# A second attention's gathers, its last tiles and its first ones: who issues, who sums, and in what order

## The reference

```python
kv_scores, indices = _pk(x, Wq_pk, pk_keys)      # per token and head: 16 best of 128 x 128 product keys, and their softmax
ind = indices + offsets[None, None, :, None]     # offsets = head * 128 * 128
k = jnp.einsum('bnhk,bnhkd->bnhd', kv_scores, keys_table[ind])
v = jnp.einsum('bnhk,bnhkd->bnhd', kv_scores, values_table[ind])
sim = jnp.einsum('bihd,bjhd->bhij', q, k)        # q is scaled by 128 ** -0.5
sim = jnp.where(causal, sim, neg)
attn = jax.nn.softmax(sim, axis=-1)
out = jnp.einsum('bhij,bjhd->bhid', attn, v)     # then heads side by side, times Wo, added to x
```

## Time and profile before

| | us |
|---|---|
| median of 3 runs | 2843.3 (2838.46, 2843.3, 2846.46) |
| the profiled execution, device time | 2838.24 |
| its span, first to last instruction | 2836.3 |
| mean granted TensorE clock | 0.932 of full speed |

### The profile page before, as it was taken

The page is one execution under the profiler, slowest core; times in us unless marked ns, Lnnn a source line. Parts: engine busy times, 40 slices in busy tenths (PEclk is TensorE's granted clock), DMA queues, the critical chain, the costliest instruction groups (busy, mean ns, idle before and its releaser), DMA issues. The chain is left out here.

```text
span 2836.3 us, 47902 instructions
## 1 busy us (share of the span) xinstructions
PE 2195.5 (77%) x11489; PEld 1773.8 (63%) x11489; DVE 1867.1 (66%) x6336; ACT 783.3 (28%) x2063; POOL 1931.2 (68%) x2033
## 2 busy tenths in 40 slices
PE   6948678887788777886878767877788777877777
PEld 6948556766566556665666655665566655665565
DVE  6689777766666666657566665656666666666541
ACT  5746422221122212221222212221223112221222
POOL 0003767777777777777777777777777777777773
PEclk8969889999999899999899899998999989989999
DMA  4301333333333333333333333333333333333332
GB/s 154 108 1 30 91 95 108 111 108 108 107 111 108 109 108 111 107 108 109 107 110 109 109 107 111 109 110 107 108 110 108 109 108 110 108 109 107 107 108 74
DMA packets 116173, 293.47 MB, mean 103 GB/s; under 512 B 37600, under 2 KB 49248, under 8 KB 113792
## 3 DMA queue, kind: packets, MB, share of 16 engines
q0 software_dynamic: 96816, 264.50, 32.6%
q1 hardware_dynamic: 14880, 23.22, 2.5%
q10 hardware_dynamic: 4144, 2.17, 0.3%
HBM read 288.69 MB, written 1.05 MB: 102 GB/s over the span
## 5 line engine op out<-in xcount | busy, mean ns | idle before, releaser
L321 POOL DMA_INDIRECT ring<-table,rows x2017 | 1923.6, 954 | 707.4 <-issue 578.3
L1565 PE MATMUL ps<-ring,staged 128*128 128x256 f32 x4096 | 995.8, 400 | 191.0 <-DMA ring<-table,rows 169.8
L1565 PEld LDWEIGHTS ps<-ring,staged 128*128 128x128 f32 x4096 | 806.0, 200 | 355.4 <-DMA ring<-table,rows 212.1
L807 DVE RECIPROCAL prec<-psum_row 128x1 f32<-128x1 f32 x128 | 21.0, 164 | 502.1 <-DVEq L806 501.8
L1641 PE MATMUL ps<-s2w,work 128*128 128x128 f32 x2176 | 306.2, 288 | 34.6 <-PEq L1639 33.8
L1177 ACT ACTIVATE work<-ps 128x256 f32<-128x256 f32 x128 | 49.0, 383 | 978.6 <-ACTq L1175 978.6
L1641 PEld LDWEIGHTS ps<-s2w,work 128*128 128x128 f32 x2176 | 274.3, 198 | 64.7 <-issue 61.2
L1610 PE MATMUL ps<-work,qT 128*128 128x512 f32 (+3 forms) x576 | 242.8, 552 | 70.4 <-PEq L1602 67.0
L799 DVE TENSOR_REDUCE nmax<-ps 128x1 f32<-128x128 f32 (+7 forms) x127 | 162.7, 1281 | 204.2 <-DVEq L798 203.5
L792 DVE TENSOR_TENSOR staged<-ps,wgt 128x2048 f32<-128x2048 f32 x128 | 292.0, 2281 | 0.2 <-issue 0.2
L1628 PE MATMUL ps<-ident,work 128*128 128x128 f32 x1088 | 189.8, 298 | 41.9 <-PEq L1551 21.7
(11 more groups left out here) (246 smaller groups left out, 2583.3 us busy)
## 6 DMA issues: line engine op xcount, KB each, us to landing
ring<-table SPq DMA_DIRECT2D x3968, 1.0 KB
ring<-table,rows POOLq DMA_INDIRECT x2017, 2.7
staged<-adj_in SPq DMA_DIRECT2D x16, 1024.0 KB, 4.8
xs<-x_in SPq DMA_DIRECT2D x4, 256.0 KB, 6.6
wpkq<-w_pkq ACTq DMA_DIRECT2D x7, 128.0 KB
out<-xs SPq DMA_DIRECT2D x1, 832.0 KB, 4.8
keyd<-pk_keys ACTq DMA_DIRECT2D x14, 32.0 KB
wo<-w_o ACTq DMA_DIRECT2D x7, 64.0 KB, 2.0
```

The costliest lines, as they stand in the source:

```text
L321: nc.gpsimd.indirect_dma_start(ring[:, t % RING, k, :], None, table_d, bass.IndirectOffsetOnAxis(ap=rows[:, t % ROWS, k:k + 1], axis=0),). ...
L1565: ins = m.matmul(to, diag(t)[:, k, :], ring[:, t % RING, k, :], start=(k == 0), stop=(k == TOPK - 1))
```

## The change

It has five parts.

1. GpSimd issues all 16 gathers of every tile, in one loop over all heads. `fetch_rows`, `turn_offsets`, `offsets_out`, `rowl` and `offs` go. The sixteenth gather of tile 15 counts on a semaphore of its own (`last_in`), so the waits have the same totals in each head.
2. SP issues the weight loads of heads 1 to 7, in place of ScalarE. It waits for `head_used` (ScalarE, in the projection of tile 15) and for `wo_used` (VectorE, as before).
3. At the start ScalarE does `elu_exp(3)` and `exp_best(3)` ahead of `kv_out(0)`, and the projection of tile 5 and the keys of tile 0 ahead of the rest of groups 3 and 4. TensorE does step 0's work right behind the sum of tile 0, then groups 3 and 4. VectorE does `spread(1)` between `elu_in(4)` and `elu_out(4)`.
4. In the last head tiles 14 and 15 are summed by VectorE: for each k one instruction multiplies the gathered rows by the token's weight and adds the sum so far, which stands in PSUM (`weighted`). There is no spread for them.
5. Tile 15's softmax is done in two parts. The past 1920 columns get their own maximum, exponential, turned blocks and product with the output weights; the own 128 columns follow with the maximum of all, and both results are added to the residual with factors that bring them to one scale (`old_scale`, `f_past`, `f_own`). The results leave in three DMAs.

```diff
@@ SP
+            with sp.Fori(1, HEADS) as h:
+                sp.wait_ge(head_used, 1)
+                sp.sem_inc(head_used, -1)
+                load_head(h)
+                sp.wait_ge(wo_used, 1)
+                sp.sem_inc(wo_used, -1)
+                sp.dma_start(wo[:, :], wo_d[h]).then_inc(wo_in, 16)
...
@@ GpSimd
-                for k in range(TOPK - by_rows(t, first)):
+                for k in range(TOPK):
...
@@ VectorE
             elu_in(4)
-            elu_out(4)
-            normal(4)
...
+            spread(1)
+            elu_out(4)
             weigh(AHEAD - 1)
+            normal(4)
             v.drain()
-            for t in range(T):
+            for t in range(1, T):
                 step(t, True, False)
...
+            def weighted(t, q):
+
+                landed(t, q)
+                for k in range(q * QK, (q + 1) * QK):
+                    w, row = wgt[:, t % 4, k:k + 1], ring[:, t % RING, k, :]
+                    if t == T - 1 and k == TOPK - 1:
+                        dve.wait_ge(last_in, 16 * HEADS)
+                    if k == 0:
+                        v.tensor_scalar(end_ps, row, w, None, ALU.mult)
+                    elif k < TOPK - 1:
+                        v.scalar_tensor_tensor(end_ps, row, w, end_ps, ALU.mult, ALU.add)
+                    else:
+                        v.scalar_tensor_tensor(kv[:, t, :], row, w, end_ps, ALU.mult, ALU.add).then_inc(kv_full, 1)
+                    v.drain()
...
+            for t in range(T - 2):
                 step(t, False, True)
+            add_out(T - 4)
+            weighted(T - 2, 0)
+            score_max(T - 3)
+            for q in range(1, QUARTERS):
+                weighted(T - 2, q)
+            score_max(T - 2)
+            add_out(T - 3)
+            dve.sem_inc(out_ready, 1)
+            weighted(T - 1, 0)
             dve.wait_ge(s_full, 1)
             dve.sem_inc(s_full, -1)
+            v.reduce_max(max_past, ps[:, 4:8, :].rearrange("p b n -> p (b n)")[:, 0:(T - 1) * P], X,
+                         negate=True).then_inc(nmax_full, 1)
+            weighted(T - 1, 1)
+            weighted(T - 1, 2)
+            add_out(T - 2)
+            dve.sem_inc(out_ready, 1)
+            weighted(T - 1, 3)
...
@@ ScalarE
+            elu_exp(3)
+            exp_best(AHEAD - 1)
             kv_out(0)
-            for g in (3, 4):
-                elu_exp(g)
-                norm_root(*GROUPS[g])
-                rows_in(g)
-                group_out(g)
...
+                softmax(t - 2)
+                turned_out(t - 2, PARITY[t - 2], t - 1)
+                softmax(t - 1)
+                turned_block(t - 1, PARITY[t - 1], 0)
+                turned_block(t - 1, PARITY[t - 1], 1)
+                act.wait_ge(nmax_full, 1)
+                act.sem_inc(nmax_full, -1)
+                s.activation(row[:, 0:past], scored[:, 0:past], ACT.Exp, bias=max_past, accum_out=sum_past).then_inc(prob_full, 1)
+                turned_block(t - 1, PARITY[t - 1], 2)
+                turned_block(t - 1, PARITY[t - 1], 3)
+                output_turned()
...
+            project_out(AHEAD + 1)
+            key_out(0)
+            norm_root(*GROUPS[3])
+            rows_in(3)
+            elu_exp(4)
+            group_out(3)
+            norm_root(*GROUPS[4])
+            rows_in(4)
+            group_out(4)
...
@@ TensorE
+            def last_steps():
+                t = T - 2
+                exponentials()
+                past_scores(t)
+                values(t - 1, PARITY[t - 1], bank1, key=t)
+
+                t = T - 1
+                exponentials()
+                past_scores(t).then_inc(s_full, 1)
+                values(t - 1, PARITY[t - 1], bank1)
+                exponentials()
+                turn_block(t - 1, PARITY[t], 0, t)
+                bank1()
+                for b in range(3):
+                    turn_block(t - 1, PARITY[t], b + 1, t)
+                    sum_block(t - 1, PARITY[t], b)
+                kv_copied()
+                turn_keys(t, ps[:, 0, 2 * P:3 * P])
+                sum_block(t - 1, PARITY[t], 3).then_inc(ot_full, 1)
+                pe.wait_ge(kt_sb, 1)
+                pe.sem_inc(kt_sb, -1)
+                own_scores(t)
+                output(t)
...
+            project(AHEAD + 1)
+            kv_copied()
+            turn_keys(0)
+            scores(0)
+            group(3)
+            group(4)
```

More of the change, by code:

```diff
@@ L45 @@
 ROWS = 2 * RING
[L46 to L51, removed]
 ROW_SLOTS = (3, 6)
@@ L260, in _ @@
             sp.dma_start(wo[:, :], wo_d[0]).then_inc(wo_in, 16)
[L261 to L273, removed]
-            for t in range(T):
[L276 to L281, removed]
+            with sp.Fori(1, HEADS) as h:
[5 more added lines that the diff above has]
+                sp.dma_start(wo[:, :], wo_d[h]).then_inc(wo_in, 16)
             sp.wait_ge(out_ready, 1)
             o = out_d.rearrange("(t p) d -> p t d", p=P)
-            sp.dma_start(o[:, 0:T - 3, :], xs[:, 0:T - 3, :]).then_inc(out_done, 16)
+            sp.dma_start(o[:, 0:T - 2, :], xs[:, 0:T - 2, :]).then_inc(out_done, 16)
             sp.wait_ge(out_ready, 2)
-            sp.dma_start(o[:, T - 3:T, :], xs[:, T - 3:T, :]).then_inc(out_done, 16)
-            sp.wait_ge(out_done, 32)
+            sp.dma_start(o[:, T - 2, :], xs[:, T - 2, :]).then_inc(out_done, 16)
+            sp.wait_ge(out_ready, 3)
+            sp.dma_start(o[:, T - 1, :], xs[:, T - 1, :]).then_inc(out_done, 16)
+            sp.wait_ge(out_done, 48)
         @block.gpsimd
@@ L323, in gather @@
                         bass.IndirectOffsetOnAxis(ap=rows[:, t % ROWS, k:k + 1], axis=0),
-                    ).then_inc(gathered[t % RING][k // QK], 16)
-            for t in range(T):
-                gather(t, True)
-            with pool.Fori(1, HEADS):
+                    ).then_inc(last_in if t == T - 1 and k == TOPK - 1 else gathered[t % RING][k // QK], 16)
+            with pool.Fori(0, HEADS):
                 for t in range(T):
-                    gather(t, False)
+                    gather(t)
         @block.vector
@@ L938, in _, with landed @@
                     step(t, False, False)
-            for t in range(T):
-                step(t, False, True)
+            def landed(t, q):
+                per = [16 * (QK - (q == QUARTERS - 1 and s == T - 1)) for s in range(t % RING, T, RING)]
+                dve.wait_ge(gathered[t % RING][q], (HEADS - 1) * sum(per) + sum(per[:t // RING + 1]))
+            def weighted(t, q):
[11 more added lines that the diff above has]
+                    v.drain()
@@ L1282, in step @@
+            def step(t, first, last):
                 if not (last and t >= T - AHEAD + 1):
@@ L1692, in step @@
                         bank1()
-                    sums(h, t, range(QUARTERS), first)
+                    sums(h, t)
                     exponentials()
```

309 lines of the change are left out of this document (146 added, 163 removed).

## The result

The changed kernel takes 2861.8 us (median of four runs, 2860.4 to 2862.2), the kernel before in the same measurement 2842.1 us (four runs, 2838.5 to 2846.5). The ratio is **1.0068, with a 95% interval of 1.0050 to 1.0085**: slower by 0.7%, 19.7 us between the medians, where 17.5 were forecast. The profiled execution took 2862.03 us; its span is 2858.9, which is 22.6 us more than the span of 2836.3 before, at a mean granted clock of 0.926 against 0.932.

A forecast was written before the change was run, and what follows sets the result against it. GpSimd's back-to-back gathers were taken as the bound from 381 to 2802 us. Gathers +37.5, start -7.7 and end -12.3 sum to +17.5 us: 2860.8 us on the median, 0.6% slower, range 2850 to 2871.

The forecast's parts named there:

- 30 gathers on the path: GpSimd before tile 13 of the last head: 30 of SyncE's 31 gathers each cost a full 1.25 us step, +37.5 us.
- the step itself: GpSimd's gather step stays at 1.25 us when SyncE's row DMAs go: neither gain nor loss, 0 us.
- start: Before tile 5's first gather: the new order shrinks GpSimd's hole from 8.02 to 0.3 us, 7.7 us earlier.
- end: From tile 13's landing in the last head to the kernel's end: 58.3 us instead of 70.65, 12.3 less.
- The 31st gather: Tile 15's last gather in the last head lands at 40.0 us after tile 13's landing, early enough to be free.
- weight loads on SyncE: Weight loads of later heads queued on SyncE behind two waits: cost 0, as they are needed 20 us after being freed.
- Scores of tile 13 end as before, at 12.3: TensorE in the last head: tile 13's scores end 12.3 us after its landing, unchanged by the edit.
- VectorE's additions: Sums of tiles 14 and 15: 0.5 us per addition (0.35 to 0.7), hidden from TensorE and not delaying GpSimd.
- Faster because the transfer counts: Gathers: rival that moving rows between queues costs nothing, so 20.0 us gained, 2823.3 us; chance 0.06.
- End bound by the last gather: End: rival that TensorE's chain is shorter and the last gather binds, 21.3 us saved, +8.5 in all; chance 0.12.
- Tile 5 still waits: Start: rival that ScalarE's new order holds up the third group's normalization and the 7.7 us stay, +25.2; chance 0.10.
- The clock falls again: End: rival that TensorE's clock drops at tile 15's past scores and the own block, +22 us, 2865.3; chance 0.10.

The follow-up runs named there:

- e7: Kernel before with only part 1 (GpSimd issues all gathers), on a chip where before takes 2840.1 us: 2878.1 us, ratio 1.0133.
- e12: Changed kernel without the last four gathers of tile 15 in the last head: tile 13's maximum to the end 42.69 us, against 43.11 in the changed kernel.
- e8: Changed kernel with the old start (part 3 undone), against the kernel before: 2868.0 us against 2840.1, ratio 1.0096.
- e5: Changed kernel with parts 1 and 2 undone (SyncE's rows and ScalarE's weight loads back), against the kernel before: 2821.6 us against 2840.1, ratio 0.993.
- e6: Kernel before with three unused tensors more in SBUF, no instruction changed: 2838.25 us beside 2840.08 for the kernel before, one run.
- e1: Kernel before, unchanged, profiled again on a chip where engines idle between instructions: 4169.3 us against 4173.9, ratio 0.9998.
- e2: Kernel before with only part 1 (GpSimd issues all gathers), on a chip where before takes 4173.9 us: 3926.0 us, ratio 0.941.
- e9: Kernel before with only the new start (part 3), on a chip where before takes 4104.1 us: 4107.7 us, ratio 1.0005.
- e3: Changed kernel with parts 1 and 2 undone (SyncE's rows and ScalarE's weight loads back), where before takes about 4170 us: ratio 1.0004 to before.
- e4: Changed kernel with the old start (part 3 undone), on a chip where before takes 4173.9 us: 3909.1 us, ratio 0.931.
- e10: Changed kernel with tile 15's softmax in one part (part 5 undone), where before takes 4104 us: ratio 0.921 to before; tile 13's maximum to end 54.35 us.
- e11: Changed kernel with parts 1 and 2 undone, plus 14 unused TensorE products before tile 14's past scores, against the kernel before: 4095.5 us against 4104.1, ratio 0.9969.

## Why the prediction was right, point by point

The forecast was +17.5 us (2860.8 on the median of the runs shown then); measured are +19.7 on the medians (2861.8) and +22.6 between the spans of the two profiled executions. That the medians come within 2.2 us is in part luck: the profiled execution of before is the quickest of its four runs, 3.8 us under their median, while that of the changed kernel lies at its median, so the medians hide over half of the miss of 5.1 us that the terms show. In the profiled ones each can be read:

| term | forecast | measured | from |
|---|---|---|---|
| 30 gathers on the path | +37.5 | +37.5 | 30 steps of before; e7 alone: +37.4 |
| the step itself | 0 | +5.6 | GpSimd's stretch is 2427.9 long, before 2384.8: 43.1, less 37.5 |
| start | -7.7 | -7.9 | tile 5 at 372.97, before 380.83 |
| end | -12.3 | -12.6 | 58.0, before 70.65 |
| sum | +17.5 | +22.6 | spans 2858.9 and 2836.3 |

**The gathers.** Right, by 0.1 us for all 30 (e7). The reason given was right too: the step with and without SyncE's rows is 1.2504 and 1.2503. The Trainium skill (DMA: Bandwidth & Descriptors, "Issuing engines are not separate DMA queues") calls the issuing time that a second engine saves usually small relative to the DMA itself. Here it is 1.25 us a gather, against 2.8 us from issue to landing, and e7 measures what it costs as 38 us of 2840, since the issuer is the bound. The 31st gather was free, as said: the end didn't wait for it (e12). So were the weight loads on SyncE, which were never moved alone: no step of GpSimd behind tile 5 was over 1.28 us in the changed kernel.

**The start.** Right: 373.1 said, 372.97 measured, and the hole comes back when the order is undone (e8).

**The end.** The sum is right by 0.3 us, but by luck: two of its parts were wrong and cancelled. "Scores of tile 13 end as before, at 12.3" came out 2.5 us late: the maximum starts at 14.90 instead of 12.40. TensorE had waited 3.00 us instead of 1.36 for tile 13's rows and started its products at a granted clock of 0.50 (first window above), and the eight products took 3.78 instead of 1.99. I had taken the stretch ahead of the edit as untouched. It isn't the new end: e7 with the old one shows the same row (3.78 behind 3.03), e5 with SyncE's rows too (3.78 behind 3.02), and e8 nearly (3.68 behind 2.95), while before and e6, the only ones of the quick condition with the old start and the old gathers, have 1.99 behind 1.36 and 1.29. What the others share is that the gathers' phase to TensorE's work has moved; that this sets the wait is argued. The wait isn't new in itself, and its length alone doesn't settle what follows. The kernel before has 99 rows of eight such products behind a wait for gathered rows. All 52 with a wait under 1.7 us took 1.99 us; of the 27 with 2.75 us or more, 17 took longer, up to 3.78, and 10 took 1.99. The changed kernel itself has such a row one tile earlier:

```profile
2780.89 1.99 PE L1586 MATMUL ps<-ring,staged 128*128 128x256 f32 x8 [3.04 <-DMA ring<-table,rows]
```

So my zero point, tile 13 of the kernel before, was one of the short waits. With the old end behind a slow row (e7) that stretch takes 69.1 us, and against it the new end gains 11.1 us instead of 12.6.

What followed in the changed kernel was 2.8 us shorter than forecast: from the scores' end to tile 13's output copy 7.7 instead of 8.7, from tile 15's past scores to tile 14's output product 7.4 instead of 8.1, from there to the own scores 6.8 instead of 7.4, and the output 1.9 instead of 2.6. The own block took 4.6 instead of 4.2, at a granted clock of 0.77. TensorE restarted 4.1 us behind tile 13's maximum, as said, and its past scores took 4.94 (5.2 said) at a granted clock of 0.65 (near 0.5 said).

**VectorE's additions.** 0.54 us each (0.5 taken, 0.7 the upper end). The last four ended at 48.2, keys turned at 50.0: cover 1.8 us. They held up nothing.

**The step that failed** is "so neither a gain nor a loss, and I take 1.25". For the removal of SyncE's rows it is right, yet the changed kernel's step is 2.9 ns longer, 5.6 us over the 1935 steps up to tile 13's last gather. That is a little more than the whole miss of 5.1 us between the profiled executions, and it is why the last gather starts at 2838.23 and not near 2832.7. What lengthens it wasn't found. In the stretched condition the step is counted over the gathers that follow each other without a wait. The kernels with the old end have 1.2500 to 1.2504 in either condition (before, e1, e2, e6, e7, e9), those with the new end 1.2516 to 1.2533 (the changed kernel, e3, e4, e5, e8, e10; 1.2516 in e5 and e8, 1.2530 and more in their twins e3 and e4), but e11 and e12, also with the new end, have 1.2503 and 1.2499. In e3 the loops of GpSimd, VectorE and SyncE are instruction for instruction those of before. SyncE's rows (e5, e7), the issuer of the weight loads (e3, e5), the tensors' places (e6) and the start (e9) don't explain it, and a drift in time is unlikely (e5 to e8, on one chip, have 1.2516, 1.2503, 1.2503 and 1.2516, as their ends are new or old). Behind tile 5 the gather's own duration is the same to 1 ns (0.948 us); the rest stands in the 0.30 us ahead of it (0.303 before, 0.305 now).

**The rivals.** Faster because the transfer counts: fell (e7). End bound by the last gather: fell (e12). Tile 5 still waits: fell (372.97, idle 0.30). The clock falls again: not in tile 15's scores of the profiled execution, but at that very place in e3, e8 and e10. In e3 and e8 it cost 2.3 to 3.0 us, tile 14's longer scores included (about 4.5 said, with the values behind the scores). In the own block it did fall (0.77), and that took 4.6 us instead of 4.2.

## What to carry to other kernels

Where the trace shows one engine issuing back to back from end to end, its step times the number of issues is that stretch's time, and a second issuer that takes 30 of 2048 issues is worth just those 30 steps: keep it, and take the gains at the start and the end on top (e5: 0.993). Count a stretch ahead of your edit as changed when the edit shifts its phase: here a wait of TensorE grew from 1.4 to 3.0 us, and the next 3.8 us ran at half the clock, as most rows behind a wait of that length did, but not all. And measure a change of who issues on more than one chip; its sign can differ.

## What the runs showed of the hardware that I had not expected

- The same program takes 2840 us on one chip and 4104 and 4174 on two others. VectorE's and GpSimd's instructions are as long as before; the gaps between them grow (VectorE 4.7 to 1012 us of "issue"). There, part 1 turned from +1.3% to -5.9%.
- TensorE's clock behind an idle isn't settled by the idle's length. A wait of 3.04 us was followed by eight products in 1.99 us and, 20 us later, one of 3.00 us by the same products in 3.78. And 1.38 us ahead of tile 15's past scores gave 3.46 us in the changed kernel, e4, e5, e11 and e12, and 5.13 to 5.15 in e3, e8 and e10. In these three the scores of tile 14 ahead of it had also been the slow ones, 6.12 to 6.20 us instead of 4.9. Two pairs of twins (e3 and e5, e4 and e8) fall on either side.
- Identical loops on GpSimd run at 1.2500 to 1.2533 us a step, depending on something outside of them; the same program had 1.2533 in one run and 1.2516 in another (e3, e5).
